# Start-up loads, the first expert's weight requests and the last routing step of a mixture-of-experts kernel in another order

## The reference

```python
att   = softmax(gelu(gelu(emb @ W0 + b0) @ W1 + b1) @ W2 + b2)      # 32 x 8, one row per sample
agg_w = einsum('bk,koi->boi', att, weight)                          # a 64 x 64 mixing matrix per sample
c0    = einsum('boi,bih->boh', agg_w, x) + (att @ bias_k)[:, :, None]
logits = c0 @ gate_w                                                # 8 experts
w_e   = softmax of the two largest logits, on their experts
x     = x + sum over e of w_e * (c0 @ expert_w[e])                  # each row goes to 2 of 8 experts
```

## Time and profile before

| What | Value |
|---|---|
| median of 3 runs | 867.15 us (867.11 to 867.46) |
| the profiled execution | 865.47 us, its span 863.6 us |
| PE busy | 820.6 us, 95% of the span |
| DVE, ACT, POOL busy | 400.2, 222.9, 89.1 us |
| chain that ended last | PE 82%, DMA 7%, DVE 6% |
| the routing phase in the trace | first x row requested at 3.59 us, first expert product at 115.63 us |

### The profile page before, as it was taken

The page is one execution under the profiler, slowest core; times in us unless marked ns, Lnnn a source line. Parts: engine busy times, 40 slices in busy tenths (PEclk is TensorE's granted clock), DMA queues, the critical chain, the costliest instruction groups (busy, mean ns, idle before and its releaser), DMA issues.

```text
span 863.6 us, 13175 instructions
## 1 busy us (share of the span) xinstructions
PE 820.6 (95%) x4308; PEld 677.2 (78%) x4309; DVE 400.2 (46%) x920; ACT 222.9 (26%) x347; POOL 89.1 (10%) x137
## 2 busy tenths in 40 slices
PE   5988779999999999999999999999999999999985
PEld 3645468888888888888887888888898889889863
DVE  1376753142333313333133051466666656656597
ACT  2445333242333413333233152310010010001100
POOL 1000021011111011111011012122112111100000
PEclk9999879999999999999999999999999999999999
DMA  8667559656371824727246243684644653521048
GB/s 282 243 198 244 193 203 395 271 178 208 109 268 69 283 97 134 242 81 284 84 164 212 97 167 93 209 251 129 153 108 106 157 125 97 142 77 25 1 133 256
DMA packets 61220, 146.11 MB, mean 169 GB/s; under 512 B 6880, under 2 KB 23536, under 8 KB 60656
## 3 DMA queue, kind: packets, MB, share of 16 engines
q1 hardware_dynamic: 40528, 90.27, 32.3%
q0 software_dynamic: 9968, 36.19, 14.3%
q10 hardware_dynamic: 10704, 19.41, 6.0%
HBM read 97.60 MB, written 39.85 MB: 159 GB/s over the span
## 4 chain that ended last, share of the span: by engine, by line
PE 82%; DMA 7%; DVE 6%; issue 2%; ACT 2%; SPq 1%; DVEq 0%; ACTq 0%; POOL 0%; POOLq 0%
PE bank L1283 62%; PE bank L1322 6%; PE bank L1274 4%; PE bank L1331 4%; DMA c_scratch<-work 2%; PE bank L1182 1%; PE bank L1385 1%; DVE work L1117 1%; PE bank L1145 1%; DMA work<-in_expert_w 1%; PE bank L1230 1%; DMA res<-in_x 1%; DMA work<-y_scratch,pos_c 1%; PE bank L1159 1%; DMA x1p<-res 1%
## 5 line engine op out<-in xcount | busy, mean ns | idle before, releaser
L1283 PE MATMUL bank<-weights,l_hi 128*128 128x512 f32 x1696 | 524.3, 390 | 0.0
L1283 PEld LDWEIGHTS bank<-weights,l_hi 128*128 128x128 f32 x1696 | 319.6, 188 | 64.6
L1283 PE MATMUL bank<-weights,l_lo 128*128 128x512 f32 x848 | 336.2, 396 | 1.4 <-DVE l_lo L906 1.3
L1283 PEld LDWEIGHTS bank<-weights,l_lo 128*128 128x128 f32 x848 | 159.9, 189 | 34.1 <-issue 2.9
L906 DVE TENSOR_TENSOR l_lo<-bank,l_hi 128x512 fp32r<-128x512 f32 x37 | 25.6, 692 | 184.1 <-ACT l_hi L684 184.1
L938 DVE TENSOR_TENSOR weights<-work,weights 128x1024 fp32r<-128x1024 f32 x64 | 76.2, 1223 | 51.7 <-ACT weights L695 51.2
L695 ACT ACTIVATE weights<-work 128x1024 fp32r<-128x1024 f32 x64 | 65.2, 1055 | 43.2 <-DMA work<-in_expert_w 25.1
L540 POOL DMA_INDIRECT work<-c_scratch,idx x37 | 39.9, 1079 | 200.4 <-PE bank L1274 199.3
L1322 PE MATMUL bank<-conv_sb,x1p 128*128 128x128 f32 x512 | 59.8, 275 | 0.6 <-DMA x1p<-res 0.6
L1322 PEld LDWEIGHTS bank<-conv_sb,x1p 128*128 128x128 f32 x512 | 58.8, 192 | 0.9 <-DMA x1p<-res 0.8
L735 ACT ACTIVATE l_hi<-work 128x512 fp32r<-128x512 f32 x32 | 18.4, 623 | 158.1 <-PE bank L1283 157.3
(11 more groups left out here) (174 smaller groups left out, 530.9 us busy)
## 6 DMA issues: line engine op xcount, KB each, us to landing
work<-in_expert_w SPq DMA_DIRECT2D x68, 512.0 KB, 6.4
y_scratch<-work ACTq DMA_DIRECT2D x74, 256.0 KB, 2.1
res<-in_x SPq DMA_DIRECT2D x16, 512.0 KB, 14.6
c_scratch<-work SPq DMA_DIRECT2D x16, 512.0 KB, 5.4
out<-work SPq DMA_DIRECT2D x16, 512.0 KB, 4.2
res<-in_x_ph SPq DMA_DIRECT2D x14, 512.0 KB, 5.5
x1p<-res SPq DMA_DIRECT2D x112, 64.0 KB, 4.7
y_scratch<-ca SPq DMA_DIRECT2D x7, 512.0 KB, 10.1
```

The costliest lines, as they stand in the source:

```text
L1283: mm = pe.matmul(to[:, :], a[:, k, :], b[:, k, cols * HALF:(cols + 1) * HALF], start=(k == 0 and n == 0), stop=(k == HC - 1 and n == 2))
```

## The change

1. SP requests x tile 0, the second part of the constants and x tile 1 ahead of the four pieces of the mixing kernels; before, the kernels came first.
2. In the routing steps SP requests `load_raw0(it + 1)` behind the stores of step `it`, with a wait for `s_lo` of `it`. Before, it requested `load_raw0(it + 2)` there, with a wait for `s_lo` of it + 1. The wait of each row block is the same number as before; it now stands behind one more pair of stores. `s_xtl` becomes two semaphores in turn, so that two `x_t` transfers in flight don't share one.
3. In step 7, PE does `logits` behind the first `mix` and not the second, and `lists(6)` ahead of `ranks(7)`; DVE does `one_hot(6)` ahead of `route(7)`, and the last two `rest0` ahead of the copy of the list.

```diff
-            for g in range(QUAD):
-                sp.dma_start(kern_sb[g * QP:g * QP + K8, :, :], kern[g, :, :].rearrange("k (o i) -> k o i", o=QO)).then_inc(s_kern, 16)
             load_x(0)
             sp.dma_start(ca[:, mlp:CA_W], consts_a[:, mlp:CA_W]).then_inc(s_const, 16)
             load_x(1)
+            for g in range(QUAD):
+                sp.dma_start(kern_sb[g * QP:g * QP + K8, :, :], kern[g, :, :].rearrange("k (o i) -> k o i", o=QO)).then_inc(s_kern, 16)
...
-                    sp.dma_start(row(it % 2 * 2, 2), x_t[tile_rows(n), :]).then_inc(s_xtl, 16)
+                    sp.dma_start(row(it % 2 * 2, 2), x_t[tile_rows(n), :]).then_inc(s_xtl[it % 2], 16)
...
-                if it + 2 < HC:
-
-                    sp.wait_ge(s_lo, it + 1)
-                    load_raw0(it + 2)
+                if 1 <= it < HC - 1:
+
+                    sp.wait_ge(s_lo, it)
+                    load_raw0(it + 1)
...
             take_gate(it)
+            one_hot(it - 1, False)
             route(ch, it)
-            one_hot(it - 1, False)
             place(ch, it)
             one_hot(it, False)
+            for k in range(HC - 2, HC):
+                rest0(k)
...
                 mix(it, 0, 0)
+                if last:
+                    logits(it)
                 mix(it, 0, 1)
                 if not last:
                     turn_x(it + 1, 1)
-                logits(it)
+                    logits(it)
...
-                if it > 0 and not last:
+                if it > 0:
                     lists(it - 1, it == 1, False)
                 if not last:
                     gate_products(it + 1)
                 ranks(it)
-            lists(NT // 2 - 2, False, False)
             lists(NT // 2 - 1, False, True)
```

More of the change, by code:

```diff
@@ L253, in build @@
         s_gred = sem("s_gred")
-        s_xtl = sem("s_xtl")
+        s_xtl = [sem(f"s_xtl_{j}") for j in range(2)]
         s_rk = sem("s_rk")
@@ L880, in _ @@
             take_gate(it)
+            one_hot(it - 1, False)
             route(ch, it)
-            one_hot(it - 1, False)
             place(ch, it)
             one_hot(it, False)
+            for k in range(HC - 2, HC):
+                rest0(k)
             dve.wait_ge(s_list, NT // 2)
             dve.tensor_copy(idx_all[:, :], bank[7][:, 0:P]).then_inc(s_ids, 1)
-            for k in range(HC - 2, HC):
-                rest0(k)
             ch = Chain(dve, s_chB)
@@ L1153, in gate_products @@
                 if it in LOADED:
-                    pe.wait_ge(s_xtl, 16 * (LOADED.index(it) + 1))
+                    pe.wait_ge(s_xtl[it % 2], 16 * sum(n <= it and n % 2 == it % 2 for n in LOADED))
                 else:
```

## The result

| | before | changed |
|---|---|---|
| median of the runs | 867.31 us | 856.17 us (854.27, 854.70, 857.64, 857.73) |
| ratio | | 0.9871, 95% interval 0.9839 to 0.9904 |
| the profiled execution, and its span | 865.47, 863.6 us | 857.64, 855.8 us |
| PE busy | 820.6 us, 95% | 821.3 us, 96% |

Of the kernel before, three runs lay at 867.11 to 867.46, with a median of 867.15; a fourth, of 2739.82 us, was disturbed, and the ratio leaves it out though the 867.31 in the table doesn't. The changed kernel was measured again beside the experiments: ratios 0.9872 [0.9839, 0.9906] and 0.9869 [0.9837, 0.99]. The gain is 867.15 - 856.17 = 11.0 us. The forecast was 6.5 us and 860.7, range 858.5 to 864.5: the sign held, each of the three parts gave something, and the size fell out of the range, on the fast side.

The account below looks back on a forecast made before the run. Bound: a chain of waits in routing (x tile 0, then PE, ACT's copies and late stores), then PE alone from 115.63 us. 1.5 + 4.56 + 0.4 = 6.5 us off 867.15 gives 860.7 us, range 858.5 to 864.5.

Parts of the forecast that it names:

- Start-up: Routing phase's start: x tile 0 requested 1.42 us earlier, ahead of the kernel pieces; gain taken as 1.5 us.
- if the landing moves along: x tile 0's load: requested 1.42 us earlier, it lands as much earlier, at 8.72 us and not 10.14.
- the cap of 1.78: ACT's copy of the first turn: from 11.34 to 9.56 us at best, since softmax ends then; gain at most 1.78.
- Rival A: At the start, a slow stretch up to 9 us holds x tile 0, so no gain: 862.2 us; chance 0.11.
- the 1.3 us estimated by it: Queue ahead of x tile 0: 256 KB of kernel pieces on half the engines, about 1.3 us more to gain.
- Steps 1 to 6: Routing steps: no copy waits for a store, 54.33 us becomes 49.77; gain 4.56, between 3.0 and 4.6.
- The two semaphores: Waits for turned x in the routing steps: as many as before, so they cost nothing.
- Rival B: Steps 3 and 5: stores still queue behind turned x, or ACT waits for row blocks; 863.0 to 865.2 us; chance 0.11.
- rival D: Step 7: the list's copy waits for weight block 7; slower, 868.8 us if 12 us late; chance 0.03.
- Rival E: Whole kernel: no change, less than 1.7 us gained, 865.5 to 868 us; chance 0.05.
- The last step: Step 7: one-hots fill DVE's idle time, list copied at about 105.7 and not 106.08; gain 0.4, between 0.1 and 0.7.
- rival C: TensorE's clock, around the first expert products: takes back or gives about 1 us on each case; no chance of its own.

## Why the prediction was right or wrong

**Start-up: direction right, size wrong.** Foreseen 1.5, at most 1.78. In the pair of profiles 2.05; by means, step 1 begins at 40.93 in the five traces with the old order and whole pieces in which the loads of turned x weren't moved (40.01, 41.83, 40.36, 41.46, 40.98; the two others had 40.91 and 40.68) and at 37.59 in the seven with the new one and without fills (37.96, 38.09, 37.66, 37.50, 38.19, 38.06, 35.66), which is 3.3. The step that failed is "if the landing moves along": I moved the landing by the request alone and kept its 6.55 us, though the earlier trace rows had the slow stretch in it, which is now seen to go with the kernel pieces. And the cap of 1.78 took ACT's softmax as fixed; its constants sat in the same slow queue. Rival A (start-up gives nothing) is refuted by the first turn at 6.71. The Trainium skill's rule on how a transfer is split over engines (DMA: Bandwidth & Descriptors, section on why a DMA increments its semaphore by 16), weighed in the prediction, pointed the right way, and the 1.3 us estimated by it were too few against 6.55 - 3.6 = 2.95; whether it is the cause isn't shown here.

**Steps 1 to 6: right, but against one draw.** Foreseen 49.77 us; measured 49.75, and between 49.75 and 49.77 in all ten other traces with the new requests. No copy of c0 waits for a store. The foreseen 4.56 was 4.58 in the pair. That it came so close is partly luck, since what I couldn't see from one trace is how wide the old order spreads: 54.33, 53.06, 57.51, 56.28, 53.61, on the mean 54.96. The term is 5.2 on the mean, and the longest of these steps are those in which the clock fell behind the wait. The two semaphores did cost nothing, since one of them is never used. Rival B (the wait changes its name) is refuted by the ACT rows, and rival D (the list waits for a weight block) too: DVE's last remainder ran at 97.51 straight behind the one before it, and the copy of the list straight behind that. Rival E (no change) is refuted by the interval, which ends at 0.9904.

**The last step: the step that failed most.** Foreseen 0.4, measured 2.41. Of the order of the one-hots I had half, 0.4 of 0.81 at the copy of the list: `place` started 0.79 us earlier against the multiplies (5.48 us behind the first, not 6.27), where I had 0.3 to 0.7, and the remainders outlasted PE by 0.02 us (10.93 against 10.91 with them put back), not 0.2. The 1.6 us on POOL I had not seen. The prediction noted that the remainders "were behind the copy and beside the gather, so their old cover is gone", and took being beside another engine as free. The row of POOL's copy, 1.11 us for 128 numbers that a copy like it at 114.62 takes in 0.18, was in the trace of before and went unread; I had followed DVE and PE through the step, and not the engine on the path between them.

**The clock, rival C,** was placed as a spread of 1 us on each case. It took back 1.2 us between step 0 and step 1 of the profiled pair, gave 0.5 in the first slot, and moves step 1 by over 2 us from one execution to the next. On the mean it took nothing back: from step 0 to step 1 it is 10.78 us in the five traces with the old order and 10.85 in the seven with the new one. It belongs in the range with 2 us rather than 1.

**The sum.** For the profiled execution the forecast was 859.0 us, and it took 857.64: 0.55 from the start-up, 2.0 from the last step and 0.5 from the first slot on the one side, 1.7 on the other, behind the first slot, where PE waits for weight blocks at a number of changes of expert that differs between executions; that these are the 1.7 isn't shown. The median is 1.5 us lower still. On the means 3.3 + 5.2 + 2.4 = 10.9 us, against the 11.0 measured. The range fell short at its fast end: the start-up term was capped by rows of before that were themselves slowed by what the change took away, the steps were taken from one trace, and POOL's part was put at nothing. The chances, too, add up to 1 with nothing left for a time below 858.8.

## What to carry to other kernels

When an edit takes load off a queue, everything that shares the queue gets shorter: don't move a landing by its request alone, and don't keep a neighbour's row as a cap. Read the duration of each small instruction on the path against the same instruction elsewhere in the trace; one six times as long names a conflict, whose other party is what runs beside it. And put no request with a wait of its own ahead of requests that are ready, on a queue that takes them in order.

## What the runs showed of the hardware

- A POOL copy of 128 x 1 out of SBUF took 0.18 us alone, 0.58 beside DVE instructions of 0.6 us with two SBUF inputs, and 1.11 beside one of 1.2 us; an indirect gather's issue 1.11, 1.25 and 1.78 us. One PSUM input instead: 0.18 and 1.11.
- The clock fell to 0.50 behind an idle stretch of 2.37 us on PE in the middle of the steps, and stayed at 1.00 behind one of 2.13 in the kernel before. In front of the first slot it stayed up behind 2.24 us and fell behind 2.39, in two executions of one kernel. In the start-up the profile's column shows a granted clock of 1.00 while transposes run at the lower clock's pace (four of 128x128 in 1.12 us, later 0.63).
- With four transfers of 64 KB with 8 partitions each, 256 KB in all, in the queue ahead of x tile 0, the engines moved 57 to 187 GB/s from 5 to 9 us, and 392 to 418 from 9 to 14 us. With the four behind x tile 1 it was 107 to 225 from 9 to 13 us.
